# Expert block, second half: the token weights come to the rows of a block by broadcast transfers instead of products for three of four units, and the loops are written out

## The reference, cut to what matters

```python
# E = 64 experts of H = 32 hidden numbers, tokens t, model width d = 128
router_scores = softmax(xt @ Wr + br)
fs = grouped_routing_scores(router_scores)      # (tokens, experts), zero where an expert is not chosen; rows divided by sum + 1e-6
up   = einsum('td,edh->teh', xt, Wup)   + bup
gate = einsum('td,edh->teh', xt, Wgate) + bgate
h    = silu(up) * gate * fs[:, :, None]          # <- the weight of a token for an expert scales 32 hidden numbers
out  = einsum('teh,ehd->td', h, Wdown) + fs @ bdown
x    = x + out
```

## Time and profile before

| | |
|---|---|
| median of 3 runs | 1285.45 us (1280.64 to 1285.48) |
| the profiled execution | 1286.17 us, of it 1284.4 us from the first to the last instruction (span) |
| PE busy | 1130.0 us, 88% of the span |
| DVE busy | 858.0 us, 67% |
| ACT, POOL busy | 604.6 us (47%), 447.4 us (35%) |
| transfers | 28.11 MB, mean 22 GB/s |
| TensorE's granted clock | 0.957 of full speed |

### The profile page before, as it was taken

One profiled execution on the slowest core, in us unless ns is written; L12 is line 12 of the kernel. 1 busy time (PEld: TensorE's weight loads), 2 busy tenths in 40 slices (PEclk: granted clock), 3 DMA queues, 4 the chain that ended last, 5 costly groups with the idle time before them and its releaser, 6 DMA issues. The chain is left out here.

```text
span 1284.4 us, 29780 instructions
## 1 busy us (share of the span) xinstructions
PE 1130.0 (88%) x11812; PEld 726.4 (57%) x11812; DVE 858.0 (67%) x1463; ACT 604.6 (47%) x1414; POOL 447.4 (35%) x392
## 2 busy tenths in 40 slices
PE   6899999899899879989787999866996799977998
PEld 5577645577535447754346854533663264434797
DVE  3777545777445986633887833687565579988655
ACT  2666444656344669633568913401562445563000
POOL 0366500566303995411896530023442000006000
PEclk9999999999998999999998999998997989997999
DMA  3110000200001210010220000000000011100001
GB/s 76 43 39 2 1 13 17 77 1 2 2 0 38 61 45 3 2 68 16 59 64 7 4 15 13 12 4 4 4 5 2 9 23 17 21 13 1 10 28 53
DMA packets 52793, 28.11 MB, mean 22 GB/s; under 512 B 35474, under 2 KB 46268, under 8 KB 52284
## 3 DMA queue, kind: packets, MB, share of 16 engines
q1 hardware_dynamic: 52668, 26.36, 8.4%
HBM read 17.17 MB, written 1.05 MB: 14 GB/s over the span
## 5 line engine op out<-in xcount | busy, mean ns | idle before, releaser
L337 POOL TENSOR_TENSOR A_pr<-A_pr,A_rs 128x1024 f32<-128x1024 f32 x64 | 121.1, 1894 | 66.6 <-DVE A_rs L401 65.4
L391 DVE TENSOR_REDUCE A_mx<-psb 128x1 f32<-128x1024 f32 x64 | 77.8, 1216 | 20.9 <-PE psb L350 20.7
L1167 POOL TENSOR_TENSOR F_raw<-F_raw,F_rc 128x1024 f32<-128x1024 f32 x32 | 75.6, 2364 | 17.4 <-DVE F_raw L1237 16.8
L434 ACT ACTIVATE A_pr<-psb,A_nm 128x1024 f32<-128x1024 f32 x64 | 71.5, 1118 | 21.4 <-DVE A_nm L395 21.2
L361 PE MATMUL psb<-ident,A_pr 128*128 128x128 f32 x512 | 71.7, 284 | 3.2 <-POOL A_pr L337 3.1
L361 PEld LDWEIGHTS psb<-ident,A_pr 128*128 128x128 f32 x512 | 56.2, 144 | 26.0 <-POOL A_pr L337 14.6
L1930 PE MATMUL psb<-M_wd,M_gates 128*128 128x128 f32 x512 | 69.5, 279 | 0.0
L1866 PE MATMUL psb<-XL,M_wu 128*128 128x512 f32 x128 | 68.2, 615 | 1.1 <-ACT M_ST L1990 1.1
L1185 PE MATMUL psb<-F_wqkv,F_hst 128*128 128x512 f32 x128 | 63.0, 616 | 6.1 <-ACT F_hst L1248 4.5
L1869 PE MATMUL psb<-XL,M_wg 128*128 128x512 f32 x128 | 67.2, 607 | 0.0
L2173 DVE TENSOR_TENSOR M_gates<-M_hall,psb 128x512 f32<-128x512 f32 x64 | 44.0, 688 | 33.4 <-PE psb L1925 33.4
(11 more groups left out here) (353 smaller groups left out, 2926.4 us busy)
## 6 DMA issues: line engine op xcount, KB each, us to landing
F_VS<-F_V SPq DMA_DIRECT2D x62, 128.0 KB, 2.3
F_raw<-in_c_xpos_dram SPq DMA_DIRECT2D x3, 1024.0 KB, 4.8
F_wqkv<-in_L_ffn_wqkv_dram SPq DMA_DIRECT2D x3, 768.0 KB, 7.4
A_w<-in_L_attn_w_dram SPq DMA_DIRECT2D x4, 256.0 KB, 3.0
M_wu<-in_L_ffn_Wup_dram SPq DMA_DIRECT2D x16, 64.0 KB, 2.1
M_wg<-in_L_ffn_Wgate_dram SPq DMA_DIRECT2D x16, 64.0 KB, 2.1
M_wd<-in_L_ffn_Wdown_dram SPq DMA_DIRECT2D x16, 64.0 KB, 1.8
M_sel<-in_c_select_dram SPq DMA_DIRECT2D x16, 64.0 KB, 2.0
```

The lines of the kernel that those rows point to most:

```text
L337: pool.tensor_tensor(p, p, rs[:, u % 2:u % 2 + 1].broadcast_to([P, SEQ]), ALU.mult).then_inc(scaled, 1)
L391: dve.tensor_reduce(mx[:, u % 2:u % 2 + 1], sview(u), AX, ALU.max).then_inc(maxed, 1)
L434: act.activation(pr[:, u % NP, :], sview(u), ACT.Exp, bias=nm[:, u % 2:u % 2 + 1], scale=scale, accum_out=su[:, u % 2:u % 2 + 1]).then_inc ...
L1167: pool.tensor_tensor(rs[:, o, :], rs[:, o, :], rc[:, o, :], ALU.add).then_inc(unit, 1)
```

## The change

1. **Select for only one unit of four.** Blocks 0 and 1 keep four selects each. From block 2 on only unit (b, 0) has a select; its bank is now `bank[b % 2]`. Units (b, 1) to (b, 3) take the weights from SBUF.
2. **Rows by transfer.** SP first writes `FSF` (64 x 2048 f32, 512 KB) to a DRAM buffer, `fs_rows`, and waits for it. Then for each block four transfers read one row each of the buffer (tokens 512 to 2047, 6 KB) and write it to the 32 partitions of that expert: 4 x 32 x 6 KB = 768 KB a block, 14 blocks. There are four slots (`row_slots`, in buffers that are free by then). Rows of blocks 2 and 3 are issued first of all; those of block b+2 stand behind the weights of block b.
3. **Order on TensorE.** select(b+1, 0) is now issued ahead of down(b, 2), with two downs of block b still to come; before it stood ahead of the last one.
4. **Loops written out** on PE, DVE, ACT and SP; all waits are against constants.

The transfers of `wd` and `sel`, their two slots, their waits, the rounding on ACT and everything after the last down stay as they are.

```diff
+            rows_load = (rows0, rows1, rows2, rows3)
+            fs_rows = nc.dram_tensor("m_fs_rows", [E, T], F32, kind="Internal").ap()
+            SPREAD = 2
...
+                row_slots = [raw_gates[:, 2:5, :].rearrange("p a n -> p (a n)"), XL[:, CH:T],
+                             FAB[:, :, :].rearrange("p a n -> p (a n)")[:, 0:3 * CH], FAB[:, :, :].rearrange("p a n -> p (a n)")[:, 3 * CH:6 * CH]]
+
+                def rows_landed(b):
+                    return 64 * len([v for v in range(SPREAD, b + 1) if v % 4 == b % 4])
+
+                def selects_to(b):
+                    return NCH * min(b, SPREAD) + max(b - SPREAD, 0)
+
+                def select_bank(b, c):
+                    return b % 2 if b >= SPREAD else c % 2
...
                     sp.wait_ge(loaded, 16 * 6)
-                    with sp.Fori(1, PAIRS) as i:
-                        for o in range(2):
-                            sp.wait_ge(down_n, (2 * i + o - 1) * NCH)
-                            issue(sp, down_load[o], down_weights(2 * i + o, o))
+                    sp.wait_ge(chosen, 2)
+                    sp.dma_start(fs_rows, FSF).then_inc(written, 16)
+                    sp.wait_ge(written, 16)
+
+                    def rows(b):
+                        for e in range(4):
+                            sp.dma_start(row_slots[b % 4][32 * e:32 * e + 32, :], fs_rows[4 * b + e:4 * b + e + 1, CH:T].broadcast_to([EH, T - CH])).then_inc(rows_load[b % 4], 16)
+                    sp.wait_ge(fs_rdy, 1)
+                    for b in range(SPREAD, EBLK):
+                        if b == SPREAD:
+                            rows(b)
+                            rows(b + 1)
+                        sp.wait_ge(down_n, (b - 1) * NCH)
+                        issue(sp, down_load[b % 2], down_weights(b, b % 2))
+                        if b + 2 < EBLK:
+                            rows(b + 2)
...
-                    def select(u, c, o):
-                        pe.matmul(bank[c % 2], selr[:, o, :], FS2[:, cs(c)], start=True, stop=True).then_inc(fs_rdy, 1)
-
-                    def down(u, c, o):
-                        pe.wait_ge(hid, u + 1)
+                    def select(b, c):
+                        if c == 0:
+                            pe.wait_ge(picked, b + 1)
+                        if b == 0:
+                            pe.wait_ge(rest, c + 1)
+                        if b >= SPREAD:
+                            pe.wait_ge(hid, NCH * (b - 2) + 1 if b - 2 >= SPREAD else NCH * SPREAD - 1 + b % 2)
+                        elif b or c >= 2:
+                            pe.wait_ge(hid, NCH * b + c - 1)
+                        pe.matmul(bank[select_bank(b, c)], selr[:, b % 2, :], FS2[:, cs(c)], start=True, stop=True).then_inc(fs_rdy, 1)
+
+                    def down(b, c):
+                        if c == 0 and b >= 2:
+                            pe.wait_ge(down_load[b % 2], (b // 2) * 2 * 16)
+                        pe.wait_ge(hid, NCH * b + c + 1)
                         for j in range(4):
...
-                    pair(0, True)
-                    with pe.Fori(1, PAIRS) as i:
-                        pair(i, False)
-                    down(EBLK * NCH - 1, NCH - 1, 1)
+                    units = [(b, c) for b in range(EBLK) for c in range(NCH)]
+                    select(0, 0)
+                    select(0, 1)
+                    base()
+                    for u, (b, c) in enumerate(units):
+                        if b < SPREAD:
+                            if u + 2 < NCH * SPREAD:
+                                down(b, c)
+                                select(*units[u + 2])
+                                continue
+                        if c == 2 and b + 1 >= SPREAD and b + 1 < EBLK:
+                            select(b + 1, 0)
+                        down(b, c)
...
-                    with act.Fori(1, PAIRS) as i:
-                        for o in range(2):
-                            act.wait_ge(down_load[o], i * 2 * 16)
-                            act.wait_ge(fs_rdy, (2 * i + o - 1) * NCH)
-                            act.activation(selr[:, o, :], sel[:, o, :], ACT.Copy).then_inc(picked, 1)
+                    for b in range(2, EBLK):
+                        act.wait_ge(down_load[b % 2], (b // 2) * 2 * 16)
+                        act.wait_ge(fs_rdy, selects_to(b - 1))
+                        act.activation(selr[:, b % 2, :], sel[:, b % 2, :], ACT.Copy).then_inc(picked, 1)
...
+                    for b in range(EBLK):
+                        for c in range(NCH):
+                            u = NCH * b + c
+                            if u >= 2:
+                                dve.wait_ge(down_n, u - 1)
+                            if b < SPREAD or c == 0:
+                                dve.wait_ge(fs_rdy, selects_to(b) + c + 1)
+                                fs = bank[select_bank(b, c)]
+                            else:
+                                dve.wait_ge(rows_load[b % 4], rows_landed(b))
+                                fs = row_slots[b % 4][:, (c - 1) * CH:c * CH]
+                            dve.tensor_tensor(hb[:, c % 2, :], hall_of(u), fs, ALU.mult).then_inc(hid, 1)
```

More of the change, by code:

```diff
@@ L1754, in build @@
                  compared, ended, summed, spread, less, tied, counted, rstep, folded, chosen, split, rest, copied, joined, xturned, xkept,
-                 down0, down1, picked, fs_rdy, hid, down_n, totalled, inverted, normed, closed, stored) = sems(
+                 down0, down1, written, rows0, rows1, rows2, rows3, picked, fs_rdy, hid, down_n, totalled, inverted, normed, closed, stored) = sems(
                 "M0", "loaded load0 load1 load2 up_rdy gate_rdy silu gated built logit soft shifted exped scored turned lower upper kept "
                 "compared ended summed spread less tied counted rstep folded chosen split rest copied joined xturned xkept "
-                "down0 down1 picked fs_rdy hid down_n totalled inverted normed closed stored", st)
+                "down0 down1 written rows0 rows1 rows2 rows3 picked fs_rdy hid down_n totalled inverted normed closed stored", st)
             load = (load0, load1, load2)
             down_load = (down0, down1)
+            rows_load = (rows0, rows1, rows2, rows3)
+            fs_rows = nc.dram_tensor("m_fs_rows", [E, T], F32, kind="Internal").ap()
+            SPREAD = 2
             half_steps, p = [], 1
@@ L1929, in down @@
+                    def down(b, c):
+                        if c == 0 and b >= 2:
+                            pe.wait_ge(down_load[b % 2], (b // 2) * 2 * 16)
+                        pe.wait_ge(hid, NCH * b + c + 1)
                         for j in range(4):
-                            last = pe.matmul(psb[:, 4 + c, j * P:(j + 1) * P], hb[:, c % 2, j * P:(j + 1) * P], wd[:, o, :],
+                            last = pe.matmul(psb[:, 4 + c, j * P:(j + 1) * P], hb[:, c % 2, j * P:(j + 1) * P], wd[:, b % 2, :],
@@ L1931, in down @@
                                              start=False, stop=True, skip_group_check=True)
                         last.then_inc(down_n, 1)
-                    def pair(i, first):
-                        for o in range(2):
[L1936 to L1952, removed]
@@ L2164, in _ @@
                         dve.tensor_tensor(FS2[E:P, cs(c)], FSF[:, cs(c)], FS2[0:E, cs(c)], ALU.subtract).then_inc(rest, 1)
[L2166 to L2182, removed]
+                    for b in range(EBLK):
[10 more added lines that the diff above has]
+                            dve.tensor_tensor(hb[:, c % 2, :], hall_of(u), fs, ALU.mult).then_inc(hid, 1)
+                            if u == 3:
+                                dve.wait_ge(totalled, 1)
+                                dve.tensor_scalar(rden[:], psb[:, 2, 0:2 * NT], 1e-6, None, ALU.add).then_inc(inverted, 1)
+                                dve.wait_ge(inverted, 1)
+                                dve.reciprocal(rden[:], rden[:]).then_inc(inverted, 1)
                     dve.wait_ge(inverted, 2)
```

## The result

The changed kernel takes **1294.8 us** (median of 5 runs, 1291.39 to 1296.16) against 1283.95 for the kernel before (5 runs, 1280.64 to 1285.48): ratio **1.0072, interval 1.0049 to 1.0095**. It is slower. The forecast was 1294.2.

A forecast was written before the change was run, and what follows sets the result against it. Taken as bound near both TensorE's work (4.48 us a block) and the turn through the weight transfer (4.64). Sum: 9.1 - 0.8 + 0.5 = +8.8 us, against 1285.45 giving 1294.2; range 1288 to 1307.

The forecast's parts named there:

- The turn through the transfer: Last down, SP's weight issues, M_sel transfer, ACT rounding, select, downs behind it: lengthens from 4.67 to 5.32 us a block, +9.1 us.
- E to E: From the end of one block's last down to the end of the next block's: 5.32 us.
- Its terms: Parts of one turn: 0.05 + 0.42 + 2.23 + 0.31 + 0.05 + 2.26 us.
- The landing: From the issue of M_sel to ACT's start: 2.23 us taken, 2.0 as the low end.
- The last block: Block 15, with no weights behind it, runs at the pace of the product slots: -0.8 us.
- The row transfers: 0.786 MB a block take 3.9 us at 200 GB/s, done before the next weights: no cost.
- third rival: Rows queued ahead of the weights hold them up below 180 GB/s: 1301 us at 150, 1320 at 120; chance 20%.
- The start: FSF write and first eight row transfers may delay block 2's weights: 0 to 1.3 us once, 0.5 taken.
- The clock: TensorE, idle about 1.6 us each turn, keeps its full clock: nothing counted.
- The signs: Profile after: M_wd issues 5.3 us apart, TensorE idle 1.3 us or more before select, then two downs without a gap.
- The sign for rows in the way: ACT starting later than 2.3 us behind the issue of M_sel would mean rows hold up the weights.
- The rival that the turn does not bind: Weights ready in time, so the two product slots set 3.9 us a block: 1274 us; chance 8%.

The follow-up runs named there:

- e5: Kernel before, loops written out, all selects kept, no row transfers, each select two downs ahead instead of one: 1294.65 us, ratio 1.0103.
- e2: Changed kernel with the next block's select ahead of the last down instead of the last but one: 1284.99 us, ratio 1.0007.
- e4: Changed kernel with row transfers for blocks 2 to 5 alone: 1290.97 us, ratio 1.0053.
- e8: Changed kernel with select ahead of the last down and row transfers for blocks 2 to 5 alone: 1278.45 us, ratio 0.9969.
- e6: Changed kernel with three slots for the weights, issued one block earlier, and three for the products: ratio 0.9939.
- e9: Changed kernel with a third slot for the weights and row transfers for blocks 2 to 5 alone: ratio 0.9952.
- e3: Changed kernel with a third slot for the weights, issued one block earlier: 1276.99 us, ratio 0.9956.
- e1: Kernel before with its four hardware loops written out, nothing else changed: 1283.58 us, ratio 0.9996.

## Why the prediction was right

**The turn through the transfer binds, and it lengthens.** Held. E to E, 14 blocks: 5.32 forecast, 74.7/14 = 5.34 measured. e5 shows that the order alone does it; e2 that undoing the order alone takes it away.

**Its terms.** SP's answer 0.05 forecast, 0.06 measured; to the second issue 0.42 against 0.39; ACT's rounding to select 0.05 against 0.05; select and two downs 2.26 against 2.26. The landing was mis-sized in its kind: I took 2.23 from the longer issue of a written-out stretch. In ten of the 14 turns it was 1.99 to 2.12, as in the loop, and the issue itself lasted 0.43. The mean is 2.27 only because four turns were late, with an instruction packet beside each of them. Here luck helped: the +0.2 us a block that I had put into every turn, 2.5 us over the 14, stands for 3.1 us in four of them, for another reason. Without the late turns the block would have taken 5.1.

**The last block.** -0.8 forecast. The last product ended 2.75 after E(14) (2.65 forecast, 3.43 before), so 0.7 was gained. But the closing stretch, from DVE's first closing step (1286.33) to the end of the span, took 6.7 us against 1284.4 - 1278.26 = 6.1, and most of the gain is not in the span. The forecast had the wrong path here: the end does not hang on the last product. First the closing rows of before (with the earlier trace rows), then those of the changed kernel:

```profile
1277.59 1.27 POOL L2049 TENSOR_TENSOR H<-H,X 128x512 f32<-128x512 f32 x1 [96.99 <-ACT H L2028]
...
1278.88 2.96 SPq L1850 DMA_DIRECT2D out_dram<-H  x4
```

```profile
1286.23 1.32 POOL L2073 TENSOR_TENSOR H<-H,X 128x512 f32<-128x512 f32 x1 [106.17 <-ACT H L2052]
1286.33 3.19 DVE L2212 SCALAR_TENSOR_TENSOR H<-psb,M_rden,X 128x128 f32<-128x128 f32 x12
1287.57 2.35 SPq L1876 DMA_DIRECT2D out_dram<-H  x4
```

The four output transfers go in order. The first waits for POOL's step on the first 512 tokens, which follows down(15, 0) and not the last product; its issue came 3.97 us after E(14) before and 3.91 now, and from it to the end of the span it took 5.5 and 5.4. In all thirteen profiles that last stretch lies between 5.4 and 5.5 us, whatever DVE does. So the term is worth 0.15 us (1284.4 - 1274.91 = 9.49 against 1293.0 - 1283.66 = 9.34), and not 0.8.

**The row transfers.** Forecast: 3.9 us a block, a slack of 0.5 us, no cost at 200 GB/s. The rate is 220 GB/s, so 3.6 us; e4 shows no cost in the pace of this order. On the third rival: its mechanism is real, and e2 shows its point: with a turn of 4.3 us instead of 5.3, the weights stand behind rows and the block takes 0.3 us more than in e8. The Trainium skill, "SBUF — State Buffer", section "Door 1: The DMA port swizzle", gives an asymptote near 218 GB/s for a transfer onto partitions 0 to 31. The trace agrees: 221 GB/s with rows alone, 220 in e6.

**The start.** +0.5 forecast, nothing seen: M_sel of block 2 landed in 2.05 us behind the eight row transfers. E(0) came 0.5 earlier than before, as did FSF, which the change does not touch. The 512 KB write took 4.4 us, within the 3.9 to 5 forecast.

**The clock.** No cost forecast, 1.00 measured, with TensorE idle for 12 of 66 us.

**The signs.** M_wd issues 5.3 us apart, select right behind the rounding, two downs after it, VectorE's waits on downs: as forecast. TensorE's idle time was forecast too large, 1.6 us a turn and 1.3 or more ahead of select: it is 12 us in 12.4 turns, and the weight load of select waited 0.97 to 1.10 us in the turns on time (0.67 in the first). The sign for rows in the way, ACT later than 2.3 us behind M_sel, came in four turns and told nothing: e4, with no rows after block 5, shows it three times.

**Sum.** 9.3 for the blocks, -0.5 from the earlier start of the stage, -0.2 for what is left of the tail: 8.6 in the span, as measured; 8.8 was forecast. The medians differ by 10.9 us; the interval of the ratio, 6 to 12 us, holds both. That the time itself was hit to 0.6 us is in part luck: the forecast was counted from a median of 1285.45, which is 1283.95 with two more runs, and the two terms that failed, -0.8 for the last block and +0.5 for the start, nearly cancel.

**The rival that the turn does not bind** (1274) fell for the changed kernel. The pace it named for the product slots, 3.86, was a little low: products of e9 set 4.02 us a block, 2.00 for two units where I had added up 1.93. Its time is the one that e3 and e6 reach (1274 to 1277), once the turn is taken away.

## What to carry to other kernels

Before work is taken off the busiest engine, close the chain that feeds its next round: here a load that may be issued only when a slot comes free, and everything that stands between its landing and the event that frees the slot. An instruction that waits for such a load should stand as late in its engine's order as it can; moved one step earlier it blocks what is behind it, and if that frees the slot, the whole loop pays, each round. A third slot takes the load out of the chain, and here only then did the saved work show.

## What the runs showed of the hardware

- Transfers onto 32 partitions at a time, each from one DRAM row read 32 times, reach 220 GB/s with the DMA engines busy throughout (221 and 1.02 in the changed kernel from 1204 to 1208 us; with the weights among them 220 and 1.06 in e6). Reading one row many times did not make them slower than the transfers onto 64 partitions, at about 200 GB/s.
- In written-out code a load of 64 KB in 512 B pieces (M_sel, issued right behind another) now and then landed 2.7 to 3.5 us after its issue instead of 2.05. All 12 of the landings over 2.6 us in six traces had an instruction packet near them, and so had 8 of the 72 others; the loop in `Fori` had no such packet. That the packet is the cause is not shown. In e2 two more late landings had none, and stood behind row transfers. A turn that is bound by the latency of a small transfer feels both.
- In the written-out loops SP issues 0.03 to 0.06 us after the down that it waits for, in the hardware loop of before 0.18 to 0.21; the next issue follows after 0.37 to 0.40 (0.67 once each in e1 and e5) instead of 0.52.
- Four output transfers of 256 KB each end 5.4 to 5.5 us after the issue of the first, in all thirteen profiles.
